# Two-layer graph network kernel: how edge tiles are grouped into node spans, and who clears and copies around them

## The reference

```python
# layer 0: an MLP on every edge, a softmax of its logit over the edges into a node, a weighted sum
feat = jnp.concatenate([n_f[edge_src], n_f[edge_dst]], axis=1)
e_f = relu(feat @ W + b)            # three kinds of edges, W_hh, W_oo, W_ho
logit = (e_f @ W_a + b_a)[:, 0]
ex = jnp.exp(logit - m[edge_dst])   # m: maximum of a node's logits
den = jax.ops.segment_sum(ex, edge_dst, num_segments=N)
z_f = jax.ops.segment_sum((ex / den[edge_dst])[:, None] * n_f[edge_src], edge_dst, num_segments=N)
x = x + relu(concatenate([n_f, z_f], axis=1) @ W_n + b_n)   # W_hn for nodes 0..127, W_on else
# layer 1: a weighted adjacency with degrees on both sides
w_in = jax.ops.segment_sum(edge_w, dst, num_segments=n)     # row sums of the adjacency
agg = jax.ops.segment_sum(xs[src] * c[:, None], dst, num_segments=n) * lax.rsqrt(deg_in)[:, None]
x = x + relu(agg @ W + b)
```

## Time and profile before

| | us |
|---|---|
| median of 3 runs | 644.88 (642.95 to 651.94) |
| the profiled execution's own time | 645.16 |
| its span in the profile | 643.3 |
| TensorE busy (share) | 570.6 (89%) |
| VectorE busy (share) | 418.8 (65%) |
| ScalarE busy (share) | 226.6 (35%) |
| GpSimd busy (share) | 159.2 (25%) |
| span stage on TensorE, first product to last fold | 377.3 to 479.2 |
| mean granted TensorE clock | 0.938 |

### The profile page before, as it was taken

How to read it: one execution, slowest core, us unless ns; L and a number is a source line. 1 busy time by engine, 2 the same in 40 slices (tenths; PEclk the granted TensorE clock), 3 DMA queues, 4 the chain that set the end, 5 groups by cost and what they waited for, 6 DMA issues and landing times.

```text
span 643.3 us, 7799 instructions
## 1 busy us (share of the span) xinstructions
PE 570.6 (89%) x2561; PEld 369.9 (57%) x2561; DVE 418.8 (65%) x692; ACT 226.6 (35%) x281; POOL 159.2 (25%) x153
## 2 busy tenths in 40 slices
PE   3979999999999798971699959989999999679997
PEld 2768887444444343421344447756668888558885
DVE  6966467277797997785959686455653763386235
ACT  4412444995725521001010842235541622015110
POOL 3200000687653746541755000000000000021000
PEclk9989999999999989997799958799999989769999
DMA  8974832899999999997899910400007253003002
GB/s 333 391 268 157 294 99 102 302 412 409 411 415 411 381 404 415 409 411 318 293 412 409 388 59 11 166 1 2 2 1 262 100 195 99 0 1 130 1 33 98
DMA packets 43653, 144.81 MB, mean 225 GB/s; under 512 B 5408, under 2 KB 5728, under 8 KB 43616
## 3 DMA queue, kind: packets, MB, share of 16 engines
q1 hardware_dynamic: 22000, 69.22, 29.1%
q0 software_dynamic: 18432, 67.12, 26.4%
q10 hardware_dynamic: 3184, 7.99, 3.3%
HBM read 131.70 MB, written 12.62 MB: 224 GB/s over the span
## 4 chain that ended last, share of the span: by engine, by line
PE 43%; DVE 24%; DMA 16%; POOL 7%; issue 6%; DVEq 2%; ACT 2%; ACTq 1%; POOLq 0%
PE banks L1073 18%; DMA rows<-table,ids_i 11%; PE banks L1224 7%; PE banks L1165 7%; POOL rows L429 6%; DVE masked L787 6%; PE banks L1241 6%; DVE rows L765 5%; DVE rows L766 4%; PE banks L1179 3%; DMA lift<-lift_row 2%; DMA lift_row<-liftT 2%; DVE stats L664 1%; PE banks L1189 1%; DVE stage L799 1%
## 5 line engine op out<-in xcount | busy, mean ns | idle before, releaser
L429 POOL DMA_INDIRECT rows<-table,ids_i x124 | 139.1, 1122 | 182.6 <-DMA table<-stage 82.7
L1093 PE MATMUL banks<-w_raw,fT_raw 128*128 128x512 f32 x384 | 168.5, 599 | 10.5 <-DMA w_raw<-in_L_gnn_W_hn_dram 4.0
L1093 PEld LDWEIGHTS banks<-w_raw,fT_raw 128*128 128x128 f32 x384 | 73.0, 191 | 105.4 <-issue 92.3
L765 DVE TENSOR_TENSOR rows<-rows 128x1024 f32<-128x1024 f32 x62 | 75.7, 1221 | 48.0 <-DMA rows<-table,ids_i 47.7
L674 DVE TENSOR_TENSOR w_lo<-w_raw,w_hi 128x1024 fp32r<-128x1024 f32 x40 | 48.4, 1223 | 57.5 <-ACT w_hi L472 52.4
L1073 PE MATMUL banks<-w_hi,fT_hi 128*128 128x512 f32 x200 | 79.6, 398 | 4.5 <-DVE w_lo L674 3.5
L1073 PE MATMUL banks<-w_lo,fT_hi 128*128 128x512 f32 x200 | 79.1, 396 | 0.0
L1073 PE MATMUL banks<-w_hi,fT_lo 128*128 128x512 f32 x200 | 78.8, 394 | 0.0
L766 DVE SCALAR_TENSOR_TENSOR rows<-rows,wa_rep 128x1024 f32<-128x1024 f32 x62 | 76.0, 1225 | 2.1
L1136 PE MATMUL banks<-w_raw,fT_raw 128*128 128x512 f32 x128 | 56.9, 606 | 18.9 <-DVE xf L819 18.9
L472 ACT ACTIVATE w_hi<-w_raw 128x1024 fp32r<-128x1024 f32 x40 | 41.7, 1059 | 88.7 <-PE banks L1073 73.9
(11 more groups left out here) (167 smaller groups left out, 648.8 us busy)
## 6 DMA issues: line engine op xcount, KB each, us to landing
w_raw<-in_L_gnn_W_ho_dram SPq DMA_DIRECT2D x16, 512.0 KB, 7.8
table<-stage SPq DMA_DIRECT2D x32, 256.0 KB, 7.8
w_raw<-in_L_gnn_W_oo_dram SPq DMA_DIRECT2D x16, 512.0 KB, 6.9
w_raw<-in_L_gnn_W_on_dram SPq DMA_DIRECT2D x16, 512.0 KB, 6.1
w_raw<-in_L_gnn_W_hn_dram SPq DMA_DIRECT2D x16, 512.0 KB, 6.7
w_raw<-in_L_gnn_W_hh_dram SPq DMA_DIRECT2D x16, 512.0 KB, 7.4
w_raw<-in_L_gnn_W_dram SPq DMA_DIRECT2D x8, 512.0 KB, 3.4
lift<-lift_row ACTq DMA_DIRECT2D x7, 512.0 KB, 8.0
```

Of the source, the lines that this page charges most:

```text
L429: pool.indirect_dma_start(out=rows[:, slot, side, :], out_offset=None, in_=table[kind][side], in_offset=bass.IndirectOffsetOnAxis(ap=ids_i ...
L765: step(dve.tensor_tensor(rows[:, r, 0, :], rows[:, r, 0, :], rows[:, r, 1, :], ALU.add))
L1093: ins = pe.matmul(bank[j][:, :], fT_raw[:, k, m * P:(m + 1) * P], w_raw[:, c % SLOTS, n * H:(n + 1) * H], start=(k == 0), stop=(k == K - 1))
```

## The change

Two parts. **In the span stage** a span no longer takes groups of eight tiles but five fixed tiles (`HEAD`) and a loop of one tile each, with `extra + 1` rounds; at the least that makes six tiles. VectorE compares the five tiles in one instruction, the loop's tile in another, and multiplies in two in the same way; the multiply of the five waits for the compare of the five (`head_made`), that of the loop for the memset behind the loop (`tail_made`). TensorE runs four products in a row, one in a loop, and a last one behind it, which signals `span_full` itself; the product of zeros is gone. The first product opens the bank (`start=True`), and nobody clears it: `clear_bank` and `bank_clear` are gone, and TensorE waits for ScalarE's copy of span n-2 instead. A span's code takes twelve bits, not nine, two to a word, and each engine loads the seven words twice, so that it holds fourteen registers. **In stage (6)** the four columns of row sums are copied by ScalarE, between its `hn_hi` of block 0 and that of block 1, and VectorE neither waits for them nor copies them there.

```diff
@@ -307,14 +306,19 @@
-        def span_code(eng, words, sp):
-
-            code = (words[sp // 2] >> (9 * (sp % 2))) & 511
+        def span_code(eng, words, n):
+
+            sp = n % SPANS
+            code = (words[n // SPANS * WORDS + sp // 2] >> (12 * (sp % 2))) & 4095
             return eng.snap(code & 63), eng.snap(code >> 6)
-        def group_at(eng, first, i):
-
-            return eng.snap(first + i * GROUP).with_bounds(max_val=T - GROUP)
+        def eng_first(eng, first):
+
+            return eng.snap(first).with_bounds(max_val=T - HEAD)
+
+        def tile_no(eng, t):
+
+            return eng.snap(t).with_bounds(max_val=T - 1)
@@ -550,15 +554,6 @@
                 act.activation(span_sum[n % 2][0:3 * SPAN, :], bank[4 + n % 2][0:3 * SPAN, :], ACT.Copy).then_inc(span_out, 1)
-                if n + 2 < 2 * SPANS:
-                    act.wait_ge(span_out, n + 1)
-                    clear_bank(n + 2)
-
-            def clear_bank(n):
-
-                act.activation(bank[4 + n % 2][0:3 * SPAN, :].rearrange("p (a c) -> p a c", c=P),
-                               zeros[0:3 * SPAN, None, :].broadcast_to([3 * SPAN, N // P, P]), ACT.Copy).then_inc(bank_clear, 1)
-
@@ -567,9 +562,6 @@
                 if c == C_HH + 8:
                     keep_edges(1)
-                    act.wait_ge(hh_raw_done, K)
-                    for n in range(2):
-                        clear_bank(n)
@@ -626,6 +618,9 @@
                 act.activation(adjT_hi[:, s, :], adjwT[:, s, :], ACT.Copy).then_inc(adjT_hi_done, 1)
             for b in range(B):
+                if b == 1:
+                    act.wait_ge(wsum_done, 1)
+                    act.activation(wsum[:, :], bank[0][:, 0:B], ACT.Copy).then_inc(wsum_kept, 1)
                 act.wait_ge(h_pre, B + b + 1)
                 act.activation(hn_hi[:, b, :], hf[:, b, :], ACT.Relu).then_inc(hn_hi_done, 1)
@@ -747,15 +741,13 @@
                 step(dve.scalar_tensor_tensor(last, last, -float(T), first, ALU.add, ALU.add))
-                step(dve.tensor_tensor(above[:, :, :], last[:, :, None].broadcast_to([1, SPANS, 7]),
-                                       node_no[0:1, GROUP + 1:T:GROUP][:, None, :].broadcast_to([1, SPANS, 7]), ALU.is_ge))
-                step(dve.tensor_reduce(extra, above[:, :, :], AX.X, ALU.add))
+                step(dve.tensor_scalar(extra, last, -float(HEAD + 1), 0.0, ALU.add, ALU.max))
                 step(dve.tensor_scalar(first, first, -1.0, float(T), ALU.mult, ALU.add))
-                step(dve.tensor_scalar(code, extra, -float(GROUP), float(T - GROUP), ALU.mult, ALU.add))
+                step(dve.tensor_scalar(code, extra, -1.0, float(T - HEAD - 1), ALU.mult, ALU.add))
                 pairs = span_row[:, 5, :].rearrange("o (w k) -> o w k", k=2)
-                step(dve.scalar_tensor_tensor(span_row[:, 0, 0:WORDS], pairs[:, :, 1], 512.0, pairs[:, :, 0], ALU.mult, ALU.add))
+                step(dve.scalar_tensor_tensor(span_row[:, 0, 0:WORDS], pairs[:, :, 1], 4096.0, pairs[:, :, 0], ALU.mult, ALU.add))
                 dve.tensor_copy(pair_word[:, :], span_row[:, 0, 0:WORDS]).then_inc(words_ready, 1)
@@ -809,7 +801,8 @@
             dve.wait_ge(words_ready, 1)
-            words = [dve.value_load(pair_word[0:1, q:q + 1], min_val=0, max_val=512 ** 2 - 1) for q in range(WORDS)]
+            words = [dve.value_load(pair_word[0:1, q % WORDS:q % WORDS + 1], min_val=0, max_val=4096 ** 2 - 1)
+                     for q in range(2 * WORDS)]
@@ -865,19 +858,26 @@
                 if n >= 2:
                     dve.wait_ge(span_full, n - 1)
-                first, extra = span_code(dve, words, sp)
+                first, extra = span_code(dve, words, n)
                 nodes = node_all[:, sp * SPAN:(sp + 1) * SPAN]
+                head = pick_dst[slot][:, 0:HEAD, :, :]
+                at_head = bass.ds(eng_first(dve, first), HEAD)
+                dve.tensor_tensor(head[:, :, 2, :], nodes[:, None, :].broadcast_to([P, HEAD, SPAN]),
+                                  dst_q[:, at_head, None].broadcast_to([P, HEAD, SPAN]), ALU.is_equal).then_inc(head_made, 1)
                 with dve.Fori(0, extra + 1) as i:
-                    q, at_pick = group_at(dve, first, i), group_at(dve, 0, i)
-                    dve.tensor_tensor(pick_dst[slot][:, bass.ds(at_pick, GROUP), 2, :],
-                                      nodes[:, None, :].broadcast_to([P, GROUP, SPAN]),
-                                      dst_q[:, bass.ds(q, GROUP), None].broadcast_to([P, GROUP, SPAN]), ALU.is_equal)
-                step(dve.memset(span_end[:, 2 * n:2 * n + 1], 0.0))
+                    q, at_pick = tile_no(dve, first + HEAD + i), tile_no(dve, i + HEAD)
+                    dve.tensor_tensor(pick_dst[slot][:, bass.ds(at_pick, 1), 2, :], nodes[:, None, :],
+                                      dst_q[:, bass.ds(q, 1), None].broadcast_to([P, 1, SPAN]), ALU.is_equal)
+                dve.memset(span_end[:, 2 * n:2 * n + 1], 0.0).then_inc(tail_made, 1)
+                dve.wait_ge(head_made, n + 1)
+                dve.tensor_tensor(head, head[:, :, 2:3, :].broadcast_to([P, HEAD, 3, SPAN]),
+                                  col[:, at_head, 1:4, None].broadcast_to([P, HEAD, 3, SPAN]), ALU.mult)
+                dve.wait_ge(tail_made, n + 1)
                 with dve.Fori(0, extra + 1) as i:
-                    q, at_pick = group_at(dve, first, i), group_at(dve, 0, i)
-                    picks = pick_dst[slot][:, bass.ds(at_pick, GROUP), :, :]
-                    dve.tensor_tensor(picks, pick_dst[slot][:, bass.ds(at_pick, GROUP), 2:3, :].broadcast_to([P, GROUP, 3, SPAN]),
-                                      col[:, bass.ds(q, GROUP), 1:4, None].broadcast_to([P, GROUP, 3, SPAN]), ALU.mult)
+                    q, at_pick = tile_no(dve, first + HEAD + i), tile_no(dve, i + HEAD)
+                    dve.tensor_tensor(pick_dst[slot][:, bass.ds(at_pick, 1), :, :],
+                                      pick_dst[slot][:, bass.ds(at_pick, 1), 2:3, :].broadcast_to([P, 1, 3, SPAN]),
+                                      col[:, bass.ds(q, 1), 1:4, None].broadcast_to([P, 1, 3, SPAN]), ALU.mult)
                 dve.memset(span_end[:, 2 * n + 1:2 * n + 2], 0.0).then_inc(span_ready, 1)
             spread(0, w_col)
@@ -1007,8 +1007,6 @@
             for s in range(B):
                 low_of(adjT_lo, s, adjwT[:, s, :], adjT_hi, adjT_hi_done, B + s + 1, adjT_lo_done)
-            dve.wait_ge(wsum_done, 1)
-            dve.tensor_copy(wsum[:, :], bank[0][:, 0:B]).then_inc(wsum_kept, 1)
             second_h(0)
@@ -1156,16 +1154,20 @@
                 sp, slot, rows3 = n % SPANS, n % 2, slice(0, 3 * SPAN)
                 out_bank = bank[4 + n % 2]
-                first, extra = span_code(pe, words, sp)
-                pe.wait_ge(bank_clear, n + 1)
+                first, extra = span_code(pe, words, n)
+                if n >= 2:
+                    pe.wait_ge(span_out, n - 1)
                 pe.wait_ge(span_ready, n + 1)
+                def product(picks, q, opens=False):
+                    return pe.matmul(out_bank[rows3, :], picks, pick_src[:, bass.ds(tile_no(pe, q), 1), :],
+                                     start=opens, stop=True, skip_group_check=True)
+
+                for j in range(HEAD - 1):
+                    product(pick_dst[slot][:, j:j + 1, :, :], first + j, j == 0)
                 with pe.Fori(0, extra + 1) as i:
-                    q, at_pick = group_at(pe, first, i), group_at(pe, 0, i)
-                    for j in range(GROUP):
-                        pe.matmul(out_bank[rows3, :], pick_dst[slot][:, bass.ds(at_pick + j, 1), :, :],
-                                  pick_src[:, bass.ds(q + j, 1), :], start=False, stop=True, skip_group_check=True)
-                pe.matmul(out_bank[rows3, 0:B], zeros[:, rows3], node_no[:, 0:B], start=False, stop=True,
-                          skip_group_check=True).then_inc(span_full, 1)
+                    product(pick_dst[slot][:, bass.ds(tile_no(pe, i + (HEAD - 1)), 1), :, :], first + (HEAD - 1) + i)
+                product(pick_dst[slot][:, bass.ds(tile_no(pe, extra + HEAD), 1), :, :], first + extra + HEAD).then_inc(span_full, 1)
```

More of the change, by code:

```diff
@@ L18 @@
 SPAN = 40
-GROUP = 8
+HEAD = 5
 TILE_HH, TILE_OO = 2, 12
@@ L172, in build @@
         span_row, _ = sb("span_row", [1, 6, 2 * WORDS], F32, over=lift_at + T * 4)
-        above, _ = sb("above", [1, SPANS, 7], F32, over=lift_at + 3 * T * 4 - 128)
         in_reach = [sb(f"in_reach{r}", [1, SPANS, T], F16, over=rows_at + REPS * CE * 4 + r * SPANS * T * 2)[0] for r in range(2)]
@@ L734, in span_words @@
                     dve.tensor_copy(q_row[:, i0:i0 + n], node_no[0:1, t0:t0 + n])
-                dve.memset(span_row[:, :, :], 0.0)
-                step(dve.memset(above[:, :, :], 0.0))
+                step(dve.memset(span_row[:, :, :], 0.0))
                 dve.tensor_copy(lo_end, node_no[0:1, 0:N:SPAN])
@@ L1193, in _ @@
             pe.wait_ge(words_ready, 1)
```

(3 more changed lines are left out.)

2 lines of the change are left out of this document (1 added, 1 removed).

## The result

The changed kernel takes 619.02 us (median of 4 runs, 618.15 to 628.21) against 643.91 us (642.19 to 651.94, 4 runs) on the same chip: ratio 0.9636, 95% interval 0.9565 to 0.9707. I predicted 620.5 us in 612 to 630. Run again in two later sets of runs it took 618.17 us (0.9599, 0.9539 to 0.9658) and 622.19 us (0.9665, 0.9625 to 0.9706).

The account below looks back on a forecast made before the run. It took TensorE to bound the kernel (43% of the chain), with waits on VectorE at the front, in spans up to 8 and at stage (6). 645.16 + 3.8 - 5.3 - 9.2 - 14.0 = 620.5 us, range 612 to 630.

Parts of the forecast that it names:

- the copy: Start of stage (6): row sums copied by ScalarE let VectorE begin block 0's `h` at 541.6 us; -14.0 us.
- the rest: Front and span stage together: loads +3.8, serial spans -5.3, spans 8 to 25 -9.2 us.
- The loads: Front: fourteen word loads for seven on VectorE, all on the path ahead of TensorE's long run; +3.8 us.
- My fear that the gathers would take it up: Behind the front: the gathers might take up the 3.8 us shift, named as a main way to be wrong.
- TensorE's loads and the late span 0: Ahead of span 0: seven more loads on TensorE are hidden; span 0 starts some 1.5 us late, costing nothing.
- Spans 8 to 25: Span stage from span 8 on: 17 periods, 16 of them gaining, fewer products; -9.2 us (bounds -4 and -12).
- 3 x 0.22 + 0.25 + 0.5 + 0.22 = 1.6 us: TensorE's products in one span, loop hole included: 1.6 us for 2.12 + 0.07, -0.6 us a span.
- a VectorE mean of 2.7: Eight spans with four `hn_lo`: VectorE's mean period 2.7 us against TensorE's 2.5, so some +1 us comes back.
- The serial part: Span stage up to span 8's start, VectorE and TensorE in series: shorter picks, set-up and products; -5.3 us (bounds -3 and -6).
- Row sums: Start of stage (6): ScalarE's copy lets `features` start at 557.2, not 563.75 us; -14.0 us (bounds -12 and -14.7).
- That VectorE's queue takes over: Rival, span stage: VectorE at 2.9 us a span or TensorE's loop 0.5 us dearer; 630 us, chance 0.12.
- The rival of the branch within a span: Rival, span stage: TensorE's loop branch stalls 0.88 us, 52 times, 46 us; about 664 us, chance 0.03.

Follow-up runs that it names:

- the second run: The changed kernel run again unedited, the second of two later sets: 622.19 us, ratio 0.9665 to the kernel before.
- the run of the spans alone: The changed kernel with the copy of the row sums put back on VectorE, ahead of block 0's `h`: 634.71 us, 0.9833 to the kernel before.
- the four-tile kernel: The changed kernel with four fixed tiles in place of five (`HEAD = 4`): 646.68 us, 1.0026 to the kernel before.

## Why the prediction was right

The time (619.0 for 620.5) and its two halves hold, though the sum owes part of its closeness to errors that offset each other: **the copy** -14.0 predicted, -14.0 measured alone; **the rest** -10.7 predicted (3.8 - 5.3 - 9.2), -10.1 measured alone.

*The loads,* +3.8: the long run began 3.64 us later (47.83; I had said 48.0). In the median seven loads cost 3.35 us in the kernel before, and moving fourteen gave back 5 to 11 us. My fear that the gathers would take it up was unfounded.

*TensorE's loads and the late span 0,* nothing: confirmed by moving them. Span 0 started 3.2 us late (380.59 for 377.35), not 1.5.

*Spans 8 to 25,* -9.2: the fold of span 7 starts 5.6 us earlier than before (417.5 for 423.1), the last product of the folds 13.8 us earlier (465.2 for 479.0), so the stretch gives -8.2, in the second run too. The sum is near, its terms are not. The term that was mis-sized is "3 x 0.22 + 0.25 + 0.5 + 0.22 = 1.6 us", with 0.45 to 0.5 us of hole behind the loop's branch in every span. In half of the spans the last product comes without a hole, so a span takes 2.13 us there, not 2.5. Span 9's picks were ready (417.20) 1.1 us ahead of its first product, and it has no hole; span 8's (415.23) 0.5 us ahead, and it has one of 0.20. I read this as TensorE's queue working ahead during the folds when the picks are there; no run tests that by itself. Against that I had no term for the two seven-tile spans. From first compare to `span_ready` they take 3.2 and 3.5 us on VectorE, where the others take 1.5 to 2.1, and they leave holes on TensorE. The nine spans with VectorE's four `hn_lo` in them take 2.38 us each, where I had a VectorE mean of 2.7.

*The serial part,* -5.3: counted from the last logits' transpose, the last `chunk_max` starts 3.4 us sooner than before (7.28 us behind it for 10.67), and span 7's fold 5.4 us sooner (36.4 us behind it for 41.8). Without span 0's picks, which lie ahead of it, I had 2.2 and 4.9. In the run of the spans alone the 5.4 is 6.4 us, in the changed kernel's second run 2.0. The slow clock in spans 4 and 5 was not in my sum: 4.15 us a span, where the kernel before with eight products had 3.1. It took back 2.2 us there (the lead is 4.8 us at span 3's fold and 2.7 at span 5's). So the term holds in size, and varies with the clock by some 4 us from one execution to another.

*Row sums,* -14.0: the row sums' start to the end of `features` went from 42.2 us (552.92 to 595.14) to 27.5 (539.20 to 566.68), -14.7. I had TensorE take the last banks late; it did not wait. Against that its 96 products took 0.24 us each, at a mean clock of 0.94, not 0.22. My working also has a slip: 563.3 and 72 products of 0.22 us make 579, not 581, so by its own terms the part would be -16. It came out well because the written value was nearer than its terms.

*The rivals.* That VectorE's queue takes over happened only with a second round: the four-tile kernel is that rival, worse than I priced it. With one tile fewer in `HEAD` the whole gain is gone. The rival of the branch within a span did not come true. On TensorE the changed kernel's branch took this long:

```profile
L1168 PEldq COMPARE_BRANCH  x28: 64/67/232, 381.6 to 462.7; - x28
```

The Trainium skill (Runtime: NRT & Kernel Launch, Instruction fetch mechanics) has a taken branch stall on a fetch when its target lies outside the fetched window. These short loops show no such stall of 0.9 us: with it out, the nine spans gained 0.16 us each. The same section of the Trainium skill has a register load (TENSOR_LOAD) take some 200 ns, and its page describes such loads as coming from HBM; those here read an on-chip tile. They take 300 ns in the row of L804, with 0.63 us from one to the next. The run with seven loads more has 3.35 us, 0.48 a load, nearer to the 0.63 than to the 0.2.

## What to carry to other kernels

A loop with a count known on the device costs by its rounds beyond the first, on each engine that runs it: choose the fixed part so that nearly all cases need one round, even if it means a product too many (one more tile cost 0.17 us a span, one more round 1.0). Put register loads where the engine waits anyway; ahead of a producer's first output they cost some 0.5 us each (3.35 us for seven). A tiny operation behind the last products of one stage must not stand ahead of what the next stage begins with: give it to an engine, or a place, where only later blocks wait for it.

## What the runs showed that I had not expected

- ScalarE's clears of 0.60 us leave the period at full clock unchanged (2.13 us). An empty closing product of 0.17 us costs 0.12 us where TensorE bounds, and nothing in the mean of the nine spans (2.39 and 2.38), which VectorE's `hn_lo` set.
- TensorE was at the 1.2 GHz level for nearly all of 380 to 422 us in one execution of the changed kernel (mean 0.51) and for about half of it in another (0.73). While there it is busy with hardly a break, at 4.15 us a span. With it go 3.4 us between the two executions; another 4.1 us lie between them at the last logits, ahead of the span stage. Each is about as large as what the clears (2.7 us) or the closing product (4.7) add in the medians. What decides them stays open.
- No run keeps the groups of eight tiles and drops only the clears or the closing product, so how the -8.2 us of spans 8 to 25 divide between fewer products and the rest is shown only as far as the rows above go.
